# Transposing h with VectorE blocks and SBUF-to-SBUF DMAs in place of TensorE, in a fused two-layer graph kernel

## The chip, the cores and the metric

The kernel runs on one core of a Trainium2 chip. The metric is the device time of one execution in microseconds (us), as the median of several executions. A profiled execution supplies the trace; its span runs from the first to the last instruction of the core. PE is TensorE's matmul side, PEld its weight loads, DVE is VectorE, ACT is ScalarE, POOL is GpSimd, and SP is SyncE, which here only issues DMAs.

## What is computed

The input x holds 128 graphs of 128 nodes with 512 features, float32. Every graph has the same 128x128 adjacency `adj`.

```python
h = max(layernorm(x), 0)
z_l, z_g, v = h @ W_lang.T, h @ W_grav.T, h @ W_V.T
A_l = max(cosine(z_l, z_l), 0) * not_eye            # z_l normalized by its row norms
A_g = exp(-squared_distance(z_g, z_g) / (2 sigma^2)) * not_eye
K   = w_l * rownorm(A_l * adj) + (1 - w_l) * rownorm(A_g * adj)
x   = x + (K @ v) @ W_O.T
h   = max(layernorm(x), 0)
out = x + (adj * adj).T @ h + bias
```

Both similarity matrices are of the form h M h^T, with M a product of a weight and its transpose. The kernel therefore never forms z. It needs h transposed (features on the partitions) for every product of this first layer.

## The kernel before

Graphs go in groups of four (GB = 4), so there are NG = 32 groups. Every float32 operand of a matmul is split into two fp32r parts, `hi` (a copy by ScalarE) and `lo` (operand minus hi, by VectorE or GpSimd), and a product takes three passes: hi hi, hi lo, lo hi (`passes`, L185; the helper `product`, L822). So each result in PSUM is drained by a pair: ScalarE writes the hi part, VectorE subtracts it and writes the lo part.

PSUM has a ring of four banks for most results. Each result is one use of the ring. The semaphore `drained` counts uses that VectorE has emptied, in order, and `free(use)` (L811) makes TensorE wait until the use four before this one is drained.

An iteration i of the main loop does, on TensorE (L858):

- the y stage: eight blocks `y_block(a, l)` of group i, of 3, 3, 6, 6, 9, 9, 12 and 12 matmuls. They read the hi and lo parts of hT, the transposed h. Before the eighth block stand the four transposes of K of group i-1 (L834).
- the K v stage: four products `k_v` of group i-1, three matmuls each. They need the split of K transposed (`kt_lo`, L584).
- the p stage: four products of 12 matmuls with 256 columns into `p_ps`. It waits for all eight y uses to be drained (L882).
- the v stage: four products v(b) of 12 matmuls (hT times MT). Behind each v(b) the four transposes of h of graph b of group i+1 (`transposes_h`, L815) go into a ring bank. Behind v(2) come eight transposes of P (L896), which wait for `p_shifted`.
- the layer-1 stage: four products `layer1` of group i-1, three matmuls each.

So one iteration has 24 uses of the ring (PER): 8 y, 4 K v, 4 v, 4 transposed h, 4 layer 1.

VectorE's order in iteration i (L644): the eight y_lo drains, between them the row factors and `combine` of K of group i-1, four `x_stats(i+1)` (batch norm statistics of the next group's x) and `kt_lo`; then `residual(i-1)` (L588: four additions and four statistics); then for each b `v_lo(b)` and `t_lo(b)`, with the reduction to `sq` behind b = 0 and `sum_s` (L706) behind b = 2; then `output` of graphs 0, 1, 2, `similarities` (L545), `output` of graph 3 and `mask_l`.

ScalarE's order (L381): the eight y_hi copies, with `w_g_K_g` and `kt_copy` between them; `apply_norm1(i+1)` (L367: four activations that make h of the next group); two copies of p; `h2_full(i-1)` for graphs 0 and 1 (L437), which wait for GpSimd's `norm2`; then for each b the copies `v_hi(b)` and `t_hi(b)`, behind b = 0 `h2_full` of graphs 2 and 3 and `shift` (which waits for `sq`), behind b = 1 and 2 two `h2_copy` each; then the exponentials.

GpSimd's order (L312): `norm1(i+1)` (ten small steps that turn the statistics of x into scale and shift), two `add_bias(i-1)`, `norm2(i-1)` (the same ten steps for the second layer norm), `diagonal(i)`, two `add_bias`, `row_norms(i)`, and four `h2_lo(i-1)` which the layer-1 stage needs.

SP's order (L216): `load_x(i+2)`, a load of 1 MB for three slots of `x_ring`; the two small DMAs of `spread_norms(i)`; four stores of 256 KB each of group i-1.

Of the kernel before, what the change touches and what calls it, by code (L numbers as in the profile page):

```python
# [5 lines left out]
ALU = mybir.AluOpType  # L25
# [4 lines left out]

P = 128
GB = 4
SLOTS = 3
# [5 lines left out]
def gnn_pair(nc, x, adj, w_lang, w_grav, w_v, w_o, gate_logit, log_sigma, bias, out):  # L39
    B, N, D = x.shape  # L40
    assert N == P and B % GB == 0 and D % P == 0 and D <= 512 and D // P == GB
    C = D // P
# [5 lines left out]
    RN_STEPS = 2  # L48
    blk = {ac: n for n, ac in enumerate(TRI)}

    G_USES = 2 * C
    SETUP = C
    PER = G_USES + GB + 2 * GB + GB

# [3 lines left out]

    HI_PER = G_USES + 2 * GB

# [6 lines left out]
    with ExitStack() as ctx:  # L69
# [46 lines left out]
        deg = sb("deg", [P, 4, GB, 2])  # L116


        raw_l = x2[:, :, :]
# [56 lines left out]
        ln1_step, ln2_step = sem("ln1_step"), sem("ln2_step")  # L176
        h2_split_dve = sem("h2_split_dve")
        ln2_last = sem("ln2_last")
        ln2_rstd = sem("ln2_rstd")
# [9 lines left out]
        def wait_for(eng, sem, count):  # L189

            if not isinstance(count, int) or count > 0:
                eng.wait_ge(sem, count)

        block = ctx.enter_context(nc.Block())
# [3 lines left out]
        def _(sp):  # L198
# [10 lines left out]
            def spread_norms(g):  # L209
# [4 lines left out]
                sp.dma_start(rn_cols[:, :, :], rn_dram.unsqueeze(0).to_broadcast([P, P, GB])).then_inc(rn_spread, 16)  # L214

            def iteration(i, load=True, store=True, after=True):  # L216
                if load:
                    sp.wait_ge(x_loaded, 16 * i + 32)
                    if store:
                        sp.wait_ge(drained, first_use(i) + G_USES + GB)  # L220
                    else:
                        sp.wait_ge(w_split, 3 * C)
                    load_x(i + 2)
                if after:
                    spread_norms(i)
                if store:
                    store_out(i - 1, first_use(i) + PER - GB * (1 if after else 2))

# [14 lines left out]
            iteration(NG - 1, load=False, after=False)  # L243
            store_out(NG - 1, first_use(NG))
            sp.wait_ge(out_stored, 16 * GB * NG)
# [115 lines left out]
        def _(act):  # L361
# [4 lines left out]

            def apply_norm1(g, wait_free=True):  # L367
                act.wait_ge(ln1_step, LN_STEPS * (g + 1))
                if wait_free:
                    act.wait_ge(t_done, GB * g)  # L370
                for b in range(GB):
# [4 lines left out]
            def t_hi(g, b, n):  # L376
                act.wait_ge(t_done, GB * g + b + 1)
                act.activation(hT[0][:, :, b], bank(n).rearrange("p (c m) -> p c m", c=C), ACT.Copy)\
                   .then_inc(hi_ready, 1)

            def iteration(i, before=True, after=True):  # L381
# [3 lines left out]
                for a in range(C):  # L385
                    for l in range(2):
# [31 lines left out]
                for b in range(GB):  # L418
# [18 lines left out]
            def h2_full(g, b, last=False):  # L437
# [64 lines left out]
            act.activation(sig, lsig, ACT.Exp).then_inc(exp_gate, 1)  # L502
            apply_norm1(0, wait_free=False)
            lw_hi(1, side, side_hi)
            for b in range(GB):
                t_hi(0, b, SETUP + b)
            act.wait_ge(a2_step, 1)
# [14 lines left out]
        def _(dve):  # L522
# [11 lines left out]
            def x_stats(g, b0, b1):  # L534
# [108 lines left out]

            def iteration(i, before=True, after=True):  # L644
                n = 0
                hi = first_hi(i)
                for a in range(C):
                    for l in range(2):
# [32 lines left out]
                for b in range(GB):  # L681
                    hi = hi + 1
                    lo(v[1][:, b], bank(n), v[0][:, b], hi).then_inc(drained, 1)
                    n += 1
                    hi = hi + 1
# [115 lines left out]
            residual(g, 0, first_use(g) + PER - GB, last=True)  # L801
            h2_lo(g, 0)
# [7 lines left out]
        def _(pe):  # L810
# [3 lines left out]

            def transposes_h(g, b, n, use):  # L815
                pe.wait_ge(h_ready, GB * g + b + 1)
                free(use)
# [40 lines left out]
            def iteration(i, before=True, after=True):  # L858
                n, use = 0, first_use(i)

                for a in range(C):
# [27 lines left out]
                for b in range(GB):  # L889
# [4 lines left out]
                    if b == (2 if after else 0):  # L894
# [27 lines left out]
            for b in range(GB):  # L922
                transposes_h(0, b, SETUP + b, SETUP + b)
            pe.wait_ge(w_loaded["o"], 16)
# [13 lines left out]
            g = NG - 1  # L938
            use = first_use(g) + PER - GB
            pe.wait_ge(kt_split, NG)  # L940
# [28 lines left out]
```

## Time and profile before

| | |
|---|---|
| three executions | 1307.92, 1308.20, 1308.43 us; median 1308.2 |
| span of the profiled execution | 1305.4 us |
| PE busy | 1281.8 us, 98% |
| DVE, ACT, POOL busy | 71%, 54%, 47% |
| share of PE on the chain that ended last | 95% |
| DMA traffic | 80 MB, mean 61 GB/s |

The span is 2.8 us less than the median; that much lies around the profiled span. A matmul row's duration includes its latency in the array. Matmuls overlap, so their cost in a stream is the distance between two starts, or the length of a piece of the chain divided by its matmuls. The chain of work that ended last is followed backwards from the last instruction, at each step to what released it. The timeline gives starts, and the idle time and releaser in brackets.

### The profile page before, as it was taken

The numbers are of one execution on the slowest core, as the hardware profiler recorded it, in microseconds if no ns is written. First come the engines' busy times: TensorE is split into PE (matmuls) and PEld (weight loads), VectorE is DVE, ScalarE is ACT, GpSimd is POOL, SyncE is SP. The second block draws the span as 40 slices with busy tenths as digits, with TensorE's granted clock in tenths as the row PEclk, the third lists the DMA queues.
The fourth block names the chain that finished last, engine by engine and source line by source line (L and its number), as shares of the span: only waits on it lengthen the run. The fifth ranks groups of instructions, "written<-read, shape, count | busy, mean of one in ns | idle before, by whom it ended". The sixth has DMA issues, their size and how long they took to land.

```text
span 1305.4 us, 22778 instructions
## 1 busy us (share of the span) xinstructions
PE 1281.8 (98%) x6820; PEld 1094.9 (84%) x6820; DVE 924.4 (71%) x1609; ACT 708.3 (54%) x1324; POOL 610.3 (47%) x995
## 2 busy tenths in 40 slices
PE   7999999999999999999999999999999999999995
PEld 6888888888888888888888888888888888888884
DVE  5477666777666777666778666778666778666678
ACT  5445655545655545655545655545555555555534
POOL 1124555444555444455444455444455444455534
PEclk9999999999999999999999999999999999999998
DMA  5011221111221121221121221121221121221011
GB/s 204 33 31 51 73 70 43 64 68 45 72 72 40 64 72 40 72 72 40 64 72 40 72 72 40 64 72 40 72 72 41 64 71 40 72 72 51 22 41 65
DMA packets 47006, 80.02 MB, mean 61 GB/s; under 512 B 7952, under 2 KB 8080, under 8 KB 46992
## 3 DMA queue, kind: packets, MB, share of 16 engines
q1 hardware_dynamic: 46416, 79.51, 18.3%
q10 hardware_dynamic: 576, 0.33, 0.1%
q8 instruction: 8, 0.13, 0.0%
q14 instruction: 6, 0.05, 0.0%
HBM read 46.20 MB, written 33.62 MB: 61 GB/s over the span
## 4 chain that ended last, share of the span: by engine, by line
PE 95%; DVE 3%; ACT 1%; DMA 1%; issue 0%; POOL 0%; SPq 0%; DVEq 0%
PE ring L824 74%; PE p_ps L824 14%; PE ring L819 4%; PE p_ps L897 2%; PE kt_ps L837 1%; DMA h2f<-in_L_gnn_W_grav 1%; DVE x_out L642 0%; DVE hT_lo L529 0%; ACT h L373 0%; DVE bn L600 0%; DVE y_lo L746 0%; DVE x L596 0%; DVE bn L541 0%; DVE K L580 0%; DVE Lw_lo L761 0%
## 5 line engine op out<-in xcount | busy, mean ns | idle before, releaser
L529 DVE TENSOR_TENSOR v_lo<-ring,v_hi 128x512 fp32r<-128x512 f32 x128 | 88.5, 692 | 290.2 <-ACT v_hi L422 290.2
L388 ACT ACTIVATE y_hi<-ring 128x512 fp32r<-128x512 f32 x256 | 149.0, 594 | 253.1 <-PE ring L824 250.6
L264 POOL TENSOR_TENSOR ln<-bn 128x4 f32<-128x4 f32 x63 | 13.1, 208 | 546.2 <-DVE bn L541 533.1
L824 PE MATMUL ring<-hT_hi,Lw_hi 128*128 128x512 f32 x640 | 252.5, 395 | 3.1 <-DVE hT_lo L529 3.1
L824 PE MATMUL ring<-hT_hi,Lw_lo 128*128 128x512 f32 x640 | 249.7, 390 | 0.0
L824 PE MATMUL ring<-hT_lo,Lw_hi 128*128 128x512 f32 x640 | 249.1, 389 | 0.0
L824 PE MATMUL ring<-MT_hi,hT_hi 128*128 128x512 f32 x512 | 208.7, 408 | 0.0
L824 PE MATMUL ring<-MT_hi,hT_lo 128*128 128x512 f32 x512 | 201.0, 393 | 0.0
L824 PE MATMUL ring<-MT_lo,hT_hi 128*128 128x512 f32 x512 | 200.3, 391 | 0.0
L295 POOL TENSOR_TENSOR h_lo<-h2f,h_hi 128x512 fp32r<-128x512 f32 x124 | 157.9, 1295 | 57.8 <-ACT h_hi L451 57.8
L529 DVE TENSOR_TENSOR y_lo<-ring,y_hi 128x512 fp32r<-128x512 f32 x256 | 170.1, 685 | 13.2 <-ACT y_hi L388 12.8
L288 POOL TENSOR_TENSOR x_out<-x,bias_sb 128x512 f32<-128x512 f32 x128 | 163.4, 1299 | 21.4 <-DVE bn L600 19.6
L824 PE MATMUL p_ps<-y_hi,hT_lo 128*128 128x256 f32 x512 | 144.9, 283 | 0.0
L824 PE MATMUL p_ps<-y_lo,hT_hi 128*128 128x256 f32 x512 | 144.9, 283 | 0.0
L824 PE MATMUL p_ps<-y_hi,hT_hi 128*128 128x256 f32 x512 | 144.7, 283 | 0.0
L824 PEld LDWEIGHTS ring<-hT_hi,Lw_hi 128*128 128x128 f32 x640 | 120.2, 188 | 27.6 <-issue 1.9
L373 ACT ACTIVATE h<-x_ring,ln 128x512 f32 (+1 forms) x128 | 94.0, 807 | 87.9 <-POOL ln L278 87.9
L824 PEld LDWEIGHTS ring<-hT_hi,Lw_lo 128*128 128x128 f32 x640 | 120.1, 188 | 25.7
L824 PEld LDWEIGHTS ring<-hT_lo,Lw_hi 128*128 128x128 f32 x640 | 120.3, 188 | 24.2
L824 PEld LDWEIGHTS ring<-MT_hi,hT_lo 128*128 128x128 f32 x512 | 96.1, 188 | 21.5
L824 PEld LDWEIGHTS ring<-MT_lo,hT_hi 128*128 128x128 f32 x512 | 96.7, 189 | 16.5
L824 PEld LDWEIGHTS ring<-MT_hi,hT_hi 128*128 128x128 f32 x512 | 96.5, 188 | 16.3
(160 smaller groups left out, 2586.0 us busy)
## 6 DMA issues: line engine op xcount, KB each, us to landing
x_ring<-in_x SPq DMA_DIRECT2D x32, 1024.0 KB, 5.3
out<-x_out SPq DMA_DIRECT2D x128, 256.0 KB, 2.1
rn_cols<-rn_dram SPq DMA_DIRECT2D x31, 256.0 KB, 3.6
x<-in_L_gnn_W_lang SPq DMA_DIRECT2D x4, 256.0 KB, 5.5
h2f<-in_L_gnn_W_grav SPq DMA_DIRECT2D x1, 1024.0 KB, 8.9
chain<-in_L_gnn_W_O SPq DMA_DIRECT2D x1, 1024.0 KB, 12.8
x_ring<-in_L_gnn_W_V SPq DMA_DIRECT2D x1, 1024.0 KB, 14.6
rn_dram<-rn SPq DMA_DIRECT2D x31, 2.0 KB, 1.4
```

The lines of the kernel that those rows point to most:

```text
L264: pool.tensor_tensor(t[:, SUM], bn[:, :, 1], bn[:, :, 4], ALU.add).then_inc(step, 1)
L288: pool.tensor_tensor(x_out[:, b], x2[:, b], bias_sb[:, :], ALU.add).then_inc(x2b_ready, 1)
L295: pool.tensor_tensor(h2[1][:, b], h2f[:, b], h2[0][:, b].bitcast(F32), ALU.subtract)\
L373: act.activation(h[:, b], xb, ACT.Relu, bias=ln1[:, SHIFT, b:b + 1], scale=ln1[:, RSTD, b:b + 1]).then_inc(h_ready, 1)
L388: act.activation(y[0][:, a, :, l], bank(n).rearrange("p (b m) -> p b m", b=GB), ACT.Copy)\
L529: return dve.tensor_tensor(out, ps, part(hi), ALU.subtract)
L819: mm = pe.transpose(bank(n)[:, c * P:(c + 1) * P], h[:, b, c * P:(c + 1) * P], ident[:, :])
L824: mm = pe.matmul(out, lhsT, rhs, start=(k == 0), stop=(k == len(terms) - 1))
L837: mm = pe.transpose(kt_ps[:, b], K[:, b], ident[:, :])
L897: mm = pe.transpose(p_ps[:, k // 2, k % 2], P_sb[:, k // 2, k % 2], ident[:, :])
```

## The change

h of the next group is no longer transposed by TensorE inside the main loop. (Group 0 still is.)

- `normalize` replaces `apply_norm1` on ScalarE: the four activations of group i+1 stand in the y stage, two behind y_hi(5), two behind y_hi(6) and `kt_copy`.
- `turn_blocks` on VectorE: four instructions per group, each transposing one graph's 128x512 in 32x32 blocks. Two stand around `kt_lo` between y_lo(6) and y_lo(7), two behind y_lo(7). They write into the buffer of h2f, which `h2_full` uses later in the same iteration.
- `turn_h` on SP, first in the iteration: when all four blocks are ready, sixteen DMAs, each of 32 partitions by 512 elements (64 KB), which carry block row i to block column j, into the new buffer `h_turned`.
- `turned_hi` and `turned_lo` take the places of `t_hi` and `t_lo` and read `h_turned` in SBUF, not PSUM. `turned_hi(b)` waits for the DMAs and for v(b), whose operand it overwrites.
- `h2_full(i-1, 0)` waits for the sixteen DMAs of group i+1.
- `x_stats` of group i+2 moves from the y stage to the v stage: two behind `sum_s` (b = 2), two behind `turned_lo(3)`, both ahead of `output`.
- The ring has 20 uses per iteration; TensorE waits for `ht_lo` at the start of each iteration.

```diff
-    PER = G_USES + GB + 2 * GB + GB
+    PER = G_USES + GB + GB + GB
...
+        h_turned = sb("h_turned", [P, NQ, C * GB * Q])
+        h_blocks = h2f[:, :, :].rearrange("p b d -> p (b d)").rearrange("p (j e) -> p j e", j=NQ)
...
+            def turn_h(g):
+                sp.wait_ge(blocks_ready, GB * g)
+                for i in range(NQ):
+                    for j in range(NQ):
+                        sp.dma_start(h_turned[j * Q:(j + 1) * Q, i], h_blocks[i * Q:(i + 1) * Q, j])\
+                          .then_inc(turned, 16)
+
             def iteration(i, load=True, store=True, after=True):
+                if after:
+                    turn_h(i + 1)
...
+            def turned_hi(g, b):
+                if b == 0:
+                    act.wait_ge(turned, TURN * g)
+                act.wait_ge(v_done, GB * (g - 1) + b + 1)
+                act.activation(hT_columns(0, b), h_columns(b), ACT.Copy).then_inc(ht_hi, 1)
...
+                        if after and G_USES - 2 <= n < G_USES:
+                            normalize(i + 1, (n - G_USES + 2) * GB // 2)
...
-                if after:
-                    apply_norm1(i + 1)
...
                     if after:
-                        t_hi(i + 1, b, n)
-                        n += 1
+                        turned_hi(i + 1, b)
...
                 if b == 0:
                     wait_for(act, h2_split, GB * g)
+                    act.wait_ge(turned, TURN * (min(g + 2, NG - 1) if isinstance(g, int) else g + 2))
...
+            def turn_blocks(g, b):
+                if b == 0 and not (isinstance(g, int) and g < 3):
+                    dve.wait_ge(h2_split, GB * (g - 2))
+                dve.wait_ge(h_ready, GB * g + b + 1)
+                out = h_blocks.rearrange("p j (c b q) -> p c b j q", c=C, b=GB)[:, :, b]
+                dve.transpose(out, h[:, b].rearrange("p (c j q) -> p c j q", c=C, j=NQ)).then_inc(blocks_ready, 1)
+
+            def turned_lo(g, b):
+                dve.wait_ge(ht_hi, GB * (g - 1) + b + 1)
+                dve.tensor_tensor(hT_columns(1, b), h_columns(b), part(hT_columns(0, b)), ALU.subtract)\
+                   .then_inc(ht_lo, 1)
...
-                        if n == G_USES - 2:
-                            if before and after:
-                                x_stats(i + 1, 0, GB // 2)
-                            if before:
-                                kt_lo(i - 1)
-                            if before and after:
-                                x_stats(i + 1, GB // 2, GB)
-                        if not before and n == G_USES:
-                            x_stats(i + 1, 0, GB)
+                        if after and n >= G_USES - 1:
+                            turn_blocks(i + 1, 2 * (n - G_USES + 1))
+                        if before and n == G_USES - 1:
+                            kt_lo(i - 1)
+                        if after and n >= G_USES - 1:
+                            turn_blocks(i + 1, 2 * (n - G_USES + 1) + 1)
...
-                    t_lo(b, n, hi).then_inc(drained, 1 if before or b < GB - 1 else 1 + GB)
-                    n += 1
+                    turned_lo(i + 1, b)
...
                     if b == 2:
                         sum_s(i)
+                    if stats and b >= 2:
+                        x_stats(i + 2, (b - 2) * GB // 2, (b - 1) * GB // 2)
...
+            x_stats(1, 0, GB)
             iteration(0, before=False)
             iteration(1)
-            with dve.Fori(2, NG - 1) as i:
+            with dve.Fori(2, NG - 2) as i:
                 iteration(i)
+            iteration(NG - 2, stats=False)
...
                 n, use = 0, first_use(i)
-
+                wait_for(pe, ht_lo, GB * i)
...
-                    if after:
-                        transposes_h(i + 1, b, n, use + n)
-                        n += 1
```

## Rows read from the trace of the kernel before

**Rows 1.** The page: busy time of TensorE; the chain that ended last, by engine.
```profile
PE 1281.8 (98%) x6820; PEld 1094.9 (84%) x6820; DVE 924.4 (71%) x1609; ACT 708.3 (54%) x1324; POOL 610.3 (47%) x995
...
PE 95%; DVE 3%; ACT 1%; DMA 1%; issue 0%; POOL 0%; SPq 0%; DVEq 0%
```
**Rows 2.** The chain in order of time, 638 to 680 us: start us, us, what.
```profile
646.53 0.44 PE ring L819 x4
...
652.94 0.87 PE p_ps L897 x8
...
657.45 13.65 PE ring L824 x60
...
671.54 5.49 PE ring L824 x24
```
**Rows 3.** The transposes of h by their line: duration ns min/median/max.
```profile
L819 PE MATMUL ring<-ident,h x512: 270/272/299, 23.1 to 1242.2; 128*128 128x128 f32 x171
```
**Rows 4.** The timeline of PE: start us, us; the first matmul of K v.
```profile
635.15 0.39 PE L824 MATMUL ring<-v_hi,KT_hi 128*128 128x512 f32 x1
```
**Rows 5.** The timeline of DVE, 630 to 662 us: start us, us, idle before.
```profile
631.43 1.28 DVE L541 BATCH_NORM_STATS2 bn<-x_ring 128x6 f32 x2
633.29 0.69 DVE L586 TENSOR_TENSOR KT_lo<-kt_ps,KT_hi 128x512 fp32r<-128x512 f32 x1 [0.58 <-ACT KT_hi L473]
...
635.98 0.69 DVE L529 TENSOR_TENSOR y_lo<-ring,y_hi 128x512 fp32r<-128x512 f32 x1 [0.21 <-ACT y_hi L388]
...
640.16 1.28 DVE L600 BATCH_NORM_STATS2 bn<-x 128x6 f32<-128x512 f32 x2
...
648.40 1.21 DVE L693 TENSOR_REDUCE sq<-chain 128x8 f32<-128x1024 f32 x1
...
655.52 1.22 DVE L708 TENSOR_TENSOR chain<-p_ps,chain 128x1024 f32<-128x1024 f32 x1
...
658.88 1.88 DVE L642 TENSOR_TENSOR x_out<-ring,x_out 128x512 f32<-128x512 f32 x3
```
**Rows 6.** The timeline of ACT, 635 to 656 us.
```profile
638.74 2.94 ACT L373 ACTIVATE h<-x_ring,ln 128x512 f32 x4 [2.79 <-POOL ln L278]
...
644.78 1.52 ACT L444 ACTIVATE h2f<-x,ln 128x512 f32<-128x512 f32 x2 [0.37 <-POOL ln L278]
646.57 0.60 ACT L422 ACTIVATE v_hi<-ring 128x512 fp32r<-128x512 f32 x1 [0.26 <-PE ring L824]
...
649.65 1.28 ACT L456 ACTIVATE chain<-chain,sq 128x128 f32<-128x128 f32 x4 [0.59 <-DVE sq L693]
650.84 0.58 ACT L422 ACTIVATE v_hi<-ring 128x512 fp32r<-128x512 f32 x1
...
651.79 1.14 ACT L451 ACTIVATE h_hi<-h2f 128x512 fp32r<-128x512 f32 x2
```
**Rows 7.** The timeline of POOL, 641 to 648 us.
```profile
641.52 0.21 POOL L264 TENSOR_TENSOR ln<-bn 128x4 f32<-128x4 f32 x1 [0.42 <-DVE bn L600]
...
644.70 2.40 POOL L302 TENSOR_TENSOR chain<-chain,diag_of 128x1024 f32<-128x1024 f32 x1
```
**Rows 8.** The timeline of SP at the start of the span.
```profile
0.81 1.81 SPq L231 DMA_DIRECT2D x<-in_L_gnn_W_lang  x4
```
**Rows 9.** SP's stores by their line: duration of an issue, ns min/median/max.
```profile
L206 SPq DMA_DIRECT2D out<-x_out x128: 332/333/349, 113.6 to 1303.0; - x128
```
**Rows 10.** The page, DMA issues: KB each, median us from issue to landing.
```profile
x_ring<-in_x SPq DMA_DIRECT2D x32, 1024.0 KB, 5.3
out<-x_out SPq DMA_DIRECT2D x128, 256.0 KB, 2.1
...
rn_dram<-rn SPq DMA_DIRECT2D x31, 2.0 KB, 1.4
```
**Rows 11.** The chain in order of time, near both ends of the span.
```profile
74.95 11.15 PE ring L824 x48
...
1242.45 13.65 PE ring L824 x60
```

More of the change, by code:

```diff
@@ L31 @@
 P = 128
+Q = 32
 GB = 4
@@ L49, in gnn_pair @@
     blk = {ac: n for n, ac in enumerate(TRI)}
+    NQ = P // Q
+    TURN = 16 * NQ * NQ
+    assert C == NQ
     G_USES = 2 * C
     SETUP = C
-    PER = G_USES + GB + 2 * GB + GB
+    PER = G_USES + GB + GB + GB
     def first_use(i):
         return SETUP + GB + PER * i
-    HI_PER = G_USES + 2 * GB
+    HI_PER = G_USES + GB
     def first_hi(i):
@@ L177, in gnn_pair @@
         h2_split_dve = sem("h2_split_dve")
+        blocks_ready, turned = sem("blocks_ready"), sem("turned")
+        ht_hi, ht_lo = sem("ht_hi"), sem("ht_lo")
         ln2_last = sem("ln2_last")
@@ L192, in wait_for, with h_columns, hT_columns @@
                 eng.wait_ge(sem, count)
+        def h_columns(b):
+            return h_turned[:, :, :].rearrange("p i (c b q) -> p c b i q", c=C, b=GB)[:, :, b]
+        def hT_columns(part, b):
+            return hT[part][:, :, b].rearrange("p c (i q) -> p c i q", q=Q)
         block = ctx.enter_context(nc.Block())
@@ L226, in iteration @@
                 if store:
-                    store_out(i - 1, first_use(i) + PER - GB * (1 if after else 2))
+                    store_out(i - 1, first_use(i) + PER - GB)
             w_rows = w_lang.rearrange("(c p) n -> p c n", p=P)
@@ L243, in _ @@
             iteration(NG - 1, load=False, after=False)
-            store_out(NG - 1, first_use(NG))
+            store_out(NG - 1, first_use(NG) + GB)
             sp.wait_ge(out_stored, 16 * GB * NG)
@@ L365, in _, with normalize @@
             act.dma_start(bias_sb[:, :], bias.unsqueeze(0).to_broadcast([P, D])).then_inc(consts_loaded, 16)
[L367 to L371, printed above, removed]
+            def normalize(g, b0):
+                if b0 == 0:
+                    act.wait_ge(ln1_step, LN_STEPS * (g + 1))
+                    if isinstance(g, int) and g == 1:
+                        act.wait_ge(t_done, GB)
+                    elif not isinstance(g, int) or g > 1:
+                        act.wait_ge(blocks_ready, GB * (g - 1))
+                for b in range(b0, b0 + GB // 2):
                     xb = x_ring[:, bass.ds(g % SLOTS, 1), b].rearrange("p s d -> p (s d)")
@@ L374, in apply_norm1, with t_hi @@
                                    scale=ln1[:, RSTD, b:b + 1]).then_inc(h_ready, 1)
-            def t_hi(g, b, n):
-                act.wait_ge(t_done, GB * g + b + 1)
+            def t_hi(b, n):
+                act.wait_ge(t_done, b + 1)
                 act.activation(hT[0][:, :, b], bank(n).rearrange("p (c m) -> p c m", c=C), ACT.Copy)\
                    .then_inc(hi_ready, 1)
+            def turned_hi(g, b):
[3 more added lines that the diff above has]
+                act.activation(hT_columns(0, b), h_columns(b), ACT.Copy).then_inc(ht_hi, 1)
             def iteration(i, before=True, after=True):
@@ L502, in _ @@
             act.activation(sig, lsig, ACT.Exp).then_inc(exp_gate, 1)
-            apply_norm1(0, wait_free=False)
+            normalize(0, 0)
+            normalize(0, GB // 2)
             lw_hi(1, side, side_hi)
             for b in range(GB):
-                t_hi(0, b, SETUP + b)
+                t_hi(b, SETUP + b)
             act.wait_ge(a2_step, 1)
@@ L642, in output, with iteration @@
                 dve.tensor_tensor(x_out[:, b], bank(n), x_out[:, b], ALU.add).then_inc(drained, 1)
-            def iteration(i, before=True, after=True):
+            def iteration(i, before=True, after=True, stats=True):
                 n = 0
@@ L682, in iteration @@
                     hi = hi + 1
-                    lo(v[1][:, b], bank(n), v[0][:, b], hi).then_inc(drained, 1)
+                    lo(v[1][:, b], bank(n), v[0][:, b], hi)\
+                        .then_inc(drained, 1 if before or b < GB - 1 else 1 + GB)
                     n += 1
-                    hi = hi + 1
-                    t_lo(b, n, hi).then_inc(drained, 1 if before or b < GB - 1 else 1 + GB)
-                    n += 1
+                    turned_lo(i + 1, b)
                     if b == 0:
@@ L793, in _ @@
             dve.tensor_tensor(A2[1][:, :], adj2[:, :], part(A2[0][:, :]), ALU.subtract).then_inc(a2_step, 1)
+            x_stats(1, 0, GB)
             iteration(0, before=False)
             iteration(1)
-            with dve.Fori(2, NG - 1) as i:
+            with dve.Fori(2, NG - 2) as i:
                 iteration(i)
+            iteration(NG - 2, stats=False)
             iteration(NG - 1, after=False)
             g = NG - 1
-            residual(g, 0, first_use(g) + PER - GB, last=True)
+            residual(g, 0, first_use(NG), last=True)
             h2_lo(g, 0)
@@ L813, in free, with transposes_h @@
                 wait_for(pe, drained, use - BANKS + 1)
-            def transposes_h(g, b, n, use):
-                pe.wait_ge(h_ready, GB * g + b + 1)
+            def transposes_h(b, n, use):
+                pe.wait_ge(h_ready, b + 1)
                 free(use)
@@ L922, in _ @@
             for b in range(GB):
-                transposes_h(0, b, SETUP + b, SETUP + b)
+                transposes_h(b, SETUP + b, SETUP + b)
             pe.wait_ge(w_loaded["o"], 16)
@@ L938, in _ @@
             g = NG - 1
-            use = first_use(g) + PER - GB
+            use = first_use(NG)
             pe.wait_ge(kt_split, NG)
```

## The prediction

> **What bounds the kernel now.** I read the busy times first, then the chain that ended last, then one iteration in the timelines. TensorE is busy for 98% of the span and holds 95% of the chain [rows 1]. In the steady part its stream has no gap: the chain in order of time is PE alone [rows 2]. So work taken from TensorE is worth its full length, until something else is late. Group 1's y stage begins at 74.95, group 31's at 1242.45 + 2.75 (three matmuls of each of four layer-1 products come first) [rows 11]. That is 1170.2 us for 30 iterations, 39.0 us each. The span is 1305.4 us against a median of 1308.2; I work on the span and add 2.8 us at the end.
>
> I count time in an iteration from the first K v matmul (t = 0, at 635.15) [rows 4]. The y stage takes 48 matmuls at 13.65 / 60 = 0.2275 us, 10.9, plus 0.44 for the transposes of K (the hole between the two last pieces) plus half of 5.49 [rows 2]: 14.1 us. So the next y stage begins at t = 24.9 before the change.
>
> **What is removed.** The transposes of h are 16 matmuls for each of 31 groups in the loop (512 in all with group 0's) [rows 3]. Their duration is 272 ns each, but they overlap: on the chain four take 0.44 us [rows 2]. Four such fours are 1.76 us an iteration. With no new wait the period is 37.24 us, the y stage begins at t = 23.1, and the kernel takes 1308.2 - 31 x 1.76 = about 1254 us. That is the most the change can give.
>
> **The DVE transposes.** No row shows one. An ordinary DVE pass over 512 elements is issued every 0.60 us (two in 1.28, three in 1.88) [rows 5]; a pass over 1024 elements takes 1.21. The transpose reads and writes 512 elements per partition, so it is nearest to the first; I take 0.60, and 1.20 as the upper end. Nothing makes it cheaper than a plain pass, so 0.60 is also the lower end. The Trainium skill (VectorE: DVE Perf Modes, The three transpose paths) gives 311 ns for a VectorE transpose of 128x128 bf16, not of float32. Four of those would be 1.24 us, the upper end, if its fixed part came each time. No run here shows it yet.
>
> The two that stand before y_lo(7) replace statistics of the same length, and are hidden: `kt_lo` ended at 633.98, and moved behind y_lo(6) and one transpose it ends at 634.65, still 0.5 us before K v. y_lo(7) starts at t = 0.83 as before [rows 5]. The two behind it stand ahead of `residual` and move it by 1.2 us. Its last statistics ended at 641.44, t = 6.3 [rows 5]; now 7.5. GpSimd's ten steps of norm2 began then, at 641.52, and released `h2_full` at 644.78, 3.26 later [rows 6, 7]. So `h2_full` of graphs 0 and 1 can begin at t = 10.8, no longer at 9.6.
>
> **The sixteen DMAs.** They start when the last block is ready, t = 2.7. Each costs SP an issue: 0.333 us [rows 9], and four in a row took 1.81, 0.45 each [rows 8]. I take 0.38 (the issue plus a gap of 0.05), because 128 stores spread over the whole span stand against four loads at its start, and the longest of the stores is 0.349. The last is issued at 2.8 + 15 x 0.38 = 8.5. From issue to landing 2 KB took 1.4 us and 256 KB took 2.1 [rows 10]; a 64 KB one lies between, so they have landed at t = 9.9 to 10.6. A load of the same 1 MB in one DMA took 5.3 us [rows 10], so the engines aren't the limit. That is just before 10.8: the DMAs are hidden behind norm2, with 0.2 to 0.9 us to spare. At 0.45 an issue and 2.1 to land it is t = 11.7, and 0.9 us shows. The Trainium skill (DMA: Bandwidth & Descriptors, Anatomy of one DMA) puts a DMA at about 2.0 us plus bytes / 436 GB/s for the GpSimd path: by it 64 KB take 2.15 us, t = 10.65, hidden by 0.15. Its section Bandwidth warns of transfers under 64 KB as descriptor-dominated and would have one of 1 MB; sixteen small ones are the opposite.
>
> Behind the sixteen on SP stands `load_x(i+2)`, then issued at t = 8.9, landing at 14.2. VectorE's statistics of that group come at 21.8, so this is free. The spread of the norms waits for GpSimd's step behind sq, at about 17, after both. The four activations of h move to idle ScalarE time, between y_hi(5) and y_hi(7); 2.94 us [rows 6]. Two take 1.5 us beside a y block of 9 or 12 matmuls (2.0 or 2.7 us), of which the copy takes 0.6: free. ScalarE's wait of 2.79 us for norm1 goes, and norm1 has the whole y stage: free.
>
> **The path through ScalarE and VectorE.** This is where I expect the loss. A copy on ScalarE is issued every 0.49 us from PSUM, 0.57 from SBUF, an h2_full every 0.74 [rows 6].
> - ScalarE: two `h2_full` at 10.8, v_hi(0) at 12.3, turned_hi(0) at 12.8, two `h2_full` at 13.35 to 14.8.
> - VectorE: v_lo(0) at 12.9, turned_lo(0) at 13.5, the reduction to sq at 14.1; `shift` follows it by 1.25 [rows 5, 6], at 15.4. The diagonal, 2.40 us behind norm2 [rows 7], is ready at 13.2 and isn't waited for. P's transposes need `shift` by 16.7; it ends at 16.6.
> - ScalarE, back to back: v_hi(1) 16.6, turned_hi(1) 17.1, two `h2_copy` 17.65, v_hi(2) 18.8, turned_hi(2) 19.3.
> - VectorE: v_lo(2) 19.4, turned_lo(2) 20.0, sum_s 20.6 to 21.8 (1.22) [rows 5], **two statistics** to 23.0, v_lo(3) 23.0, turned_lo(3) 23.6, **two statistics** 24.2 to 25.4, output of graph 0 until 26.05.
>
> The first y block reuses the bank of layer 1 of graph 0 (four uses back), so it waits for that output, although hT's lo part is ready at 24.3. Before, the outputs stood directly behind t_lo(3): the first ended at 659.56, t = 24.4 [rows 5], 0.5 us before the y stage. That slack is gone, the y stage would be ready 1.76 us sooner, and 2.4 us of statistics are put ahead of the output. It begins at t = 26.1 rather than 23.1: a stall of 3.0 us. Part of it shows already at layer 1, whose fourth product waits for v_lo(3) until 23.7. What is queued behind these instructions on VectorE (outputs 1 and 2, similarities, output 3, mask_l) costs the fourth y block 0.1 us more. The y stage is then 14.2 and the period 40.3 us, against 39.0.
>
> **The sum.** Iteration 0 has no outputs: it loses its transposes and keeps the wait for ht_lo(3), so group 1 begins at 73.5 instead of 74.95. Twenty-nine periods of 40.3 are 1168.7. Iteration 30 has no statistics: its outputs begin at 23.0, and layer 1, waiting for h2's lo parts, ends at about 24.1; with the y stage 38.3. From there to the end nothing is changed: 1305.4 - 1245.2 = 60.2. Together 1340.7, plus 2.8: **1343.5 us**, 2.7% slower.
>
> **Rivals.**
> - **The drains aren't late** (faster). If ScalarE keeps pace with TensorE, v(3) is ready at 20.5, v_lo(3) starts at 21.2, turned_lo(3) at 21.8, the statistics at 22.4, output 0 ends at 24.2. The stall is 1.2 us, the period 38.5, the sum 1290 us. It needs ScalarE 1.8 us ahead of my schedule; its chain starts from norm2, which the moved residual makes later, so the profile speaks against it. A chance of 0.17, with 0.03 of it for no stall at all (1254).
> - **The break-even point** is a stall of 1.75 us, output 0 done at 24.85. Chance of landing there 0.04.
> - **The DMAs land late** (slower still). From t = 10.8 on, each us of lateness delays `h2_full`, v_hi(0) and everything after them by one us. At t = 11.7 to 11.9, 1 us: period 41.3, 1372 us. For it: the spacing at the start of the trace, and that no SBUF-to-SBUF transfer is in it. Chance 0.18.
> - **A DVE transpose takes two passes.** 0.6 more each: `kt_lo` ends 0.1 late for K v, y_lo(7) starts 0.4 later, residual 1.2 more. Norm2, and the DMAs too, come 1.6 us later: 29 x 1.6 = 47, 1390 us. Chance 0.13.
>
> **Range and chances.** My forecast's own case has 0.48 and reaches from 1325 to 1360 (0.5 us an iteration either way). The break-even chance is split over the three. Faster 0.18, within 0.2% 0.02, slower 0.80; 0.2% is about what a measurement of this kernel can tell from no change. For 8 in 10 the range takes in 1290 below and 1390 above and leaves the gain without a stall out.
>
> **What would show it.** In the changed profile TensorE should wait about 3 us in each of 29 iterations, mostly at the first y block, released by VectorE's output (x_out), with smaller waits at layer 1 for v_lo and h_lo. ScalarE's `h2_full` should be released by GpSimd's norm2; if it is a DMA, the DMA rival holds, and its excess is the lateness. A VectorE transpose should last about 0.68 us, issued every 0.60. SP should issue the sixteen in about 6 us. I am wrong if output 0 comes less than 1.7 us behind the last layer-1 product, if TensorE's waits sum to under 50 us, or if the DMAs' landing, not norm2, sets the start of `h2_full` by more than a us.

## The result, and the profile after

The changed kernel takes 1469.8 us (median of four, 1468.9 to 1472.0), against 1308.1 us for the kernel before: a ratio of 1.124, 95% interval 1.1225 to 1.1257. Slower was forecast, but 1343.5 us with a range from 1290 to 1390; the loss is 162 us and not 35.

The page of the changed kernel: busy times, the chain that ended last by engine, and the new DMAs (KB each, median us from issue to landing). The chain was 95% PE before [rows 1].

```profile
PE 1292.6 (88%) x6324; PEld 1065.8 (73%) x6324; DVE 1020.4 (70%) x1733; ACT 702.0 (48%) x1324; POOL 652.7 (44%) x995
...
PE 34%; SPq 18%; DVE 16%; issue 13%; ACT 12%; DMA 5%; DVEq 2%; ACTq 0%; POOL 0%
...
h_turned<-h2f SPq DMA_DIRECT2D x496, 64.0 KB, 2.0
```

SP's queue holds 18% of the chain. A queue that only issues DMAs has become a link of it. The waits of the engines (us in total, times, longest) name who waits for what:

```profile
ACT h2f L458 <- DMA h_turned<-h2f: 150.1, 30, 5.8
...
PE p_ps L923 <- ACT chain L470: 98.9, 31, 4.0
...
PE ring L850 <- DVE x_out L669: 40.8, 30, 1.4
...
PE ring L850 <- DVE v_lo L544: 7.8, 26, 0.7
```

ScalarE's `h2_full` waits for the sixteen DMAs in 30 iterations, and TensorE waits in front of the transposes of P and at the first y block. One iteration follows in the timelines of PE, SP and ACT. The first K v matmul starts at 621.50; that is t = 0.

```profile
621.50 0.39 PE L850 MATMUL ring<-v_hi,KT_hi 128*128 128x512 f32 x1
...
641.57 1.11 PE L923 MATMUL p_ps<-ident,chain 128*128 128x128 f32 x8 [3.25 <-ACT chain L470]
...
642.91 0.63 PE L850 MATMUL ring<-MT_lo,hT_hi 128*128 128x512 f32 x1
...
651.62 0.50 PE L850 MATMUL ring<-hT_hi,Lw_hi 128*128 128x512 f32 x1 [1.42 <-DVE x_out L669]
```
```profile
624.26 10.04 SPq L216 DMA_DIRECT2D h_turned<-h2f  x16
634.90 0.40 SPq L196 DMA_DIRECT2D x_ring<-in_x  x1
```
```profile
635.75 1.52 ACT L458 ACTIVATE h2f<-x,ln 128x512 f32<-128x512 f32 x2 [4.98 <-DMA h_turned<-h2f]
```

The sixteen issues start at t = 2.76, as worked out, but take 10.04 us, 0.63 each. `h2_full` starts at t = 14.25, where norm2 alone would have let it start at 10.8. The next y stage begins at t = 30.1; before the change it began at 24.9 [rows 2, 4]. The period is 44.4 us.

VectorE in the same iteration:

```profile
622.94 1.29 DVE L563 STREAM_TRANSPOSE h2f<-h 128x512 f32<-128x512 f32 x2
...
638.40 0.68 DVE L567 TENSOR_TENSOR hT_lo<-h_turned,hT_hi 128x512 fp32r<-128x512 f32 x1
...
644.68 1.57 DVE L567 TENSOR_TENSOR hT_lo<-h_turned,hT_hi 128x512 fp32r<-128x512 f32 x1
```

The block transposes cost what a plain pass costs (1.29 us for two, [rows 5] 1.28). The same `turned_lo` (hT_lo) takes 0.68 us once and, for b = 2, 1.57. The matmul at 642.91 lasts 0.63 us where others last 0.39. The row of that stretch (us busy of PE, PEld, DVE, ACT and POOL, then the granted clock as a share of full speed, the DMA share and GB/s) says why:

```profile
641.60:646.10 4.50, 4.50 (x17) 3.72 (x18) 3.31 (x4) 4.01 (x8) 3.17 (x4) 0.62 0.30 48
```

The granted clock is at its lower level (1.2 in place of 2.4 GHz) for 3.4 us in most iterations, behind TensorE's wait of 3.25 us; over these 4.5 us that makes a mean of 0.62.

### The profile page after: what moved, and what is told of

It reads as the page before. It is cut to its first block, busy times and chain, and to the rows that moved or that the text cites. A ratio compares the mean times of both kernels' runs of the same rounds, so it can differ in the third digit from the quotient of the medians.

```text
span 1468.0 us, 22296 instructions
## 1 busy us (share of the span) xinstructions
PE 1292.6 (88%) x6324; PEld 1065.8 (73%) x6324; DVE 1020.4 (70%) x1733; ACT 702.0 (48%) x1324; POOL 652.7 (44%) x995
## 4 chain that ended last, share of the span: by engine, by line
PE 34%; SPq 18%; DVE 16%; issue 13%; ACT 12%; DMA 5%; DVEq 2%; ACTq 0%; POOL 0%
PE ring L850 33%; SPq L216 18%; DVE bn L556 4%; DMA h_turned<-h2f 4%; ACT v_hi L436 3%; DVE sq L715 3%; DVE chain L732 2%; ACT h_hi L465 2%; ACT chain L470 2%; ACT h2f L458 2%; DVE h2f L563 2%; DVE x_out L669 1%; DVE hT_lo L567 1%; ACT y_hi L402 1%; ACT hT_hi L393 1%
## 5 line engine op out<-in xcount | busy, mean ns | idle before, releaser
L850 PE MATMUL ring<-hT_hi,Lw_hi 128*128 128x512 f32 x640 | 257.7, 403 | 44.3 <-DVE x_out L669 40.8
L850 PE MATMUL ring<-MT_hi,hT_hi 128*128 128x512 f32 x512 | 217.9, 426 | 0.0
L850 PE MATMUL ring<-MT_lo,hT_hi 128*128 128x512 f32 x512 | 214.1, 418 | 0.0
L850 PE MATMUL ring<-MT_hi,hT_lo 128*128 128x512 f32 x512 | 212.8, 416 | 0.0
L300 POOL TENSOR_TENSOR h_lo<-h2f,h_hi 128x512 fp32r<-128x512 f32 x124 | 172.0, 1418 | 45.2 <-ACT h_hi L465 45.2
L458 ACT ACTIVATE h2f<-x,ln 128x512 f32<-128x512 f32 x128 | 97.1, 805 | 159.1 <-DMA h_turned<-h2f 150.1
L424 ACT ACTIVATE chain<-p_ps 128x512 f32<-128x512 f32 x64 | 38.3, 598 | 230.2 <-PE p_ps L850 230.2
L923 PE MATMUL p_ps<-ident,chain 128*128 128x128 f32 x256 | 38.2, 296 | 98.9 <-ACT chain L470 98.9
L850 PEld LDWEIGHTS ring<-MT_hi,hT_lo 128*128 128x128 f32 x512 | 104.7, 205 | 23.9
L850 PEld LDWEIGHTS ring<-MT_hi,hT_hi 128*128 128x128 f32 x512 | 105.9, 207 | 21.5
```

Of the source, the lines that this page charges most:

```text
L300: pool.tensor_tensor(h2[1][:, b], h2f[:, b], h2[0][:, b].bitcast(F32), ALU.subtract)\
L424: act.activation(P_sb[:, 2 * half:2 * half + 2], p_ps[:, 2 * half:2 * half + 2], ACT.Copy)\
L850: mm = pe.matmul(out, lhsT, rhs, start=(k == 0), stop=(k == len(terms) - 1))
L923: mm = pe.transpose(p_ps[:, k // 2, k % 2], P_sb[:, k // 2, k % 2], ident[:, :])
```

## The experiments

Three theories stood against each other: the sixteen issues on one queue; the order of the work on VectorE (statistics ahead of the outputs); and VectorE and GpSimd hindering each other, or TensorE's clock.

**What an issue costs.** `e_issue` is the kernel before with small DMAs behind its end. Two of its nine groups:

```diff
+            for k in range(4):
+                sp.dma_start(dst[32:64, k], src[0:32, k]).then_inc(trial, 16)
+            landed(4)
...
+            for k in range(4):
+                sp.dma_start(trial_dram[32 * k:32 * k + 32], src[0:32, k]).then_inc(trial, 16)
+            landed(4)
```

> The kernel before with a row of small DMAs behind the last store, four of each form and then a wait until they have landed: 32 partitions by 2 KB within SBUF to another quarter of the partitions, to the same quarter, in the last quarter; 128 partitions by 512 bytes, by 2 KB and by 1 KB within SBUF; 32 partitions by 2 KB from SBUF to DRAM and back; and sixteen in the pattern of the change. The question is why an issue takes 0.59 us (0.63 apart) where a store of 128 rows takes 0.333. If the form with 32 partitions costs it, the 32-partition forms show 0.59 and those of 128 partitions 0.33. If SBUF on both sides costs it, all forms within SBUF show 0.59 and the stores to DRAM 0.33. If it is only the queue filling up, the first DMA of each four is at 0.33 and the later ones at 0.59.

SP's timeline. L257 to L269 are the first five forms, L272 goes to DRAM, L275 comes from it, L278 is the one by 1 KB, L282 the sixteen:

```profile
1305.82 2.56 SPq L257 DMA_DIRECT2D h<-x_ring  x4
1309.82 2.43 SPq L260 DMA_DIRECT2D h<-x_ring  x4
1313.71 2.90 SPq L263 DMA_DIRECT2D h<-x_ring  x4
1318.07 2.47 SPq L266 DMA_DIRECT2D h<-x_ring  x4
1321.91 2.44 SPq L269 DMA_DIRECT2D h<-x_ring  x4
1326.29 1.77 SPq L272 DMA_DIRECT2D trial_dram<-x_ring  x4
1329.38 1.70 SPq L275 DMA_DIRECT2D h<-trial_dram  x4
1332.59 2.43 SPq L278 DMA_DIRECT2D h<-x_ring  x4
1336.54 10.09 SPq L282 DMA_DIRECT2D h<-x_ring  x16
```

Every form within SBUF takes about 0.61 us an issue (one group of four 0.73), whether 32 or 128 partitions, 64 or 256 KB, and sixteen in a row take 0.63 each. With DRAM on one side it is 0.43 to 0.44, for the same 32 partitions by 2 KB. So SBUF on both sides costs it, not the shape. The rows of single issues show a second, smaller effect: the first of a burst is cheap (0.312 and 0.366 us with DRAM, 0.49 to 0.54 within SBUF), the later ones are not (0.42 and 0.59 to 0.60). The 0.333 us of the stores [rows 9] were issues that each stood alone.

**Eight issues on each of two queues.**

```diff
-                for i in range(NQ):
+                for i in range(NQ // 2):
...
+            def turn_half(g):
+                act.wait_ge(blocks_ready, GB * g)
+                for i in range(NQ // 2, NQ):
+                    for j in range(NQ):
+                        act.dma_start(h_turned[j * Q:(j + 1) * Q, i], h_blocks[i * Q:(i + 1) * Q, j])\
+                           .then_inc(turned, 16)
...
+                if after:
+                    turn_half(i + 1)
```

> The changed kernel with eight of the sixteen DMAs issued by ScalarE's queue (between its last y copy and its first copy of p) and eight by SP. Theory 1, the issue on one queue: sixteen issues 0.63 us apart land the blocks at t = 14.2 (t counted from the first K v matmul), 3.4 us after norm2 releases h2_full at 10.8; with eight they land at about 2.8 + 7 x 0.63 + 2.0 = 9.2, the wait of h2_full on the DMAs (150 us in total) goes, each of 29 periods falls from 44.4 by about 3.4 to 4.1 us, and so do TensorE's waits in front of the transposes of P; 1470 - 29 x 3.8 = about 1360 us, and the low clock in each iteration disappears too. Rival A, the DMA engines themselves are slow with 32-partition transfers: the landing comes no earlier than before, and the time stays near 1470. Rival B, the lateness is set elsewhere (the statistics in front of the outputs): under 1.5 us an iteration are won, 1425 or more.

1409.9 us, ratio 1.078 (1.0758 to 1.0794): 2.0 us an iteration won, not 3.8. The cause held (`h2_full` is now released by GpSimd), the size didn't. The timelines of ACT and DVE and two pieces of the chain of this kernel (its t = 0 is at 641.76):

```profile
652.66 1.52 ACT L467 ACTIVATE h2f<-x,ln 128x512 f32<-128x512 f32 x2 [1.64 <-POOL ln L283]
```
```profile
655.31 1.40 DVE L576 TENSOR_TENSOR hT_lo<-h_turned,hT_hi 128x512 fp32r<-128x512 f32 x1
...
662.32 1.61 DVE L576 TENSOR_TENSOR hT_lo<-h_turned,hT_hi 128x512 fp32r<-128x512 f32 x1
```
```profile
625.91 12.80 PE ring L859 x48
...
669.28 11.29 PE ring L859 x48
```

`h2_full` starts at t = 10.9, as the prediction had it, 3.35 us sooner than in the changed kernel. Of that, 0.7 us goes to turned_lo(0), which now takes 1.40 us. And in 13 of 30 iterations a low stretch of the clock falls into the y stage, where nothing covers it: 48 matmuls take 12.80 us instead of 11.29. That is 1.5 us each time (2.4 in one), 0.7 on average: the periods are 41.8 us without such a stretch and 43.4 with it. 3.35 - 0.7 - 0.7 is 1.95, against 2.0 measured.

**The same megabyte in four DMAs.** `q_four` leaves out the move of the blocks to other partitions, so it doesn't compute the kernel's result; the bytes moved and the work of the compute engines are the same.

```diff
-    TURN = 16 * NQ * NQ
+    TURN = 16 * NQ
...
-                for i in range(NQ):
-                    for j in range(NQ):
-                        sp.dma_start(h_turned[j * Q:(j + 1) * Q, i], h_blocks[i * Q:(i + 1) * Q, j])\
-                          .then_inc(turned, 16)
+                for j in range(NQ):
+                    sp.dma_start(h_turned[:, j], h_blocks[:, j]).then_inc(turned, 16)
```

> The changed kernel with the sixteen DMAs of 64 KB replaced by four of 256 KB on SP, 128 partitions each: the same megabyte within SBUF with four issues. The blocks are not moved to other partitions, so the transposed h is wrong and the output isn't the reference's; the work of every engine is as before. If the number of issues (0.63 us each within SBUF) made the landing late, the blocks land at 2.8 + 3 x 0.63 + 2.5 = 7.2, h2_full is released by norm2 at t = 10.8, and the first y block starts at t = 26.1 of the prediction plus 1.4 for two turned_lo that run beside GpSimd: about 27.5, period 41.7, 1385 us, and up to 1410 with the lower clock that the run with two queues still had. If the megabyte itself is slow within SBUF, h2_full still waits for the DMAs and the time stays near 1470.

1408.2 us, ratio 1.077 (1.0755 to 1.0791), the same as with two queues, and within what was expected. The bytes are equal, the issues take 2.42 us instead of 10.04, and the wait for the DMAs is gone. With `e_issue`, where 32 and 128 partitions cost the same, this settles it: the number of issues on one queue made the landing late, not the megabyte, and ScalarE's part in `a_split` costs nothing.

```profile
641.69 2.42 SPq L215 DMA_DIRECT2D h_turned<-h2f  x4
```
```profile
649.83 1.52 ACT L456 ACTIVATE h2f<-x,ln 128x512 f32<-128x512 f32 x2 [1.62 <-POOL ln L281]
```

**The statistics ahead of the outputs**, first with the moves alone. In `d_moves` TensorE keeps its transposes.

```diff
+                        if after and G_USES - 2 <= n < G_USES:
+                            normalize(i + 1, (n - G_USES + 2) * GB // 2)
...
-                if after:
-                    apply_norm1(i + 1)
...
-                            if before and after:
-                                x_stats(i + 1, 0, GB // 2)
...
+                    if stats and b >= 2:
+                        x_stats(i + 2, (b - 2) * GB // 2, (b - 1) * GB // 2)
```

> The kernel before with TensorE's transposes kept, and only the two moves of the change: h's activations in the y stage, and the next statistics in the v stage in front of the outputs. If the statistics in front of the outputs hold up the first y block as the prediction had it, output 0 ends at t = 26.8 instead of 24.4, the y stage begins 1.9 us late in 29 iterations: 1308 + 55 = 1363 us. If the whole loss is the DMAs', the moves cost nothing: 1308 us, and the wait of TensorE on x_out stays under 5 us in total.

1340.2 us, ratio 1.0245 (1.0228 to 1.0262): the moves alone cost 32 us, 1.1 us in each of 29 iterations. The first y block waits for output 0. DVE's v_lo(3) in the kernel before, DVE here, and a wait of PE here:

```profile
657.68 0.69 DVE L529 TENSOR_TENSOR v_lo<-ring,v_hi 128x512 fp32r<-128x512 f32 x1 [0.94 <-ACT v_hi L422]
```
```profile
673.64 0.67 DVE L530 TENSOR_TENSOR v_lo<-ring,v_hi 128x512 fp32r<-128x512 f32 x1
...
674.83 1.27 DVE L542 BATCH_NORM_STATS2 bn<-x_ring 128x6 f32 x2
676.02 1.87 DVE L643 TENSOR_TENSOR x_out<-ring,x_out 128x512 f32<-128x512 f32 x3
```
```profile
PE ring L822 <- DVE x_out L643: 21.0, 29, 0.7
```

v_lo(3) has no idle time in front of it here. In the kernel before, VectorE waited 0.94 us there for ScalarE; the first two statistics fill that hole. 1.9 expected less 0.9 is 1.0: the y stage begins 0.9 us later than before, and it takes 0.2 us more itself.

`b_split_stats` moves the statistics of the two-queue kernel out of that place. The edit against `a_split`:

```diff
-                    if stats and b >= 2:
-                        x_stats(i + 2, (b - 2) * GB // 2, (b - 1) * GB // 2)
+                    if stats and b < 2:
+                        x_stats(i + 2, b * GB // 2, (b + 1) * GB // 2)
```

> As the one before (eight DMAs on each of two queues), and the four statistics of the group after next stand on VectorE behind sq (b = 0) and behind turned_lo(1), where VectorE waits anyway, not in front of the outputs. Theory 1 with the prediction's second term, that 2.4 us of statistics ahead of output 0 hold up the first y block: the period falls by another 2.4 us, to about 38.5, and the kernel takes about 1290 us, below the kernel before. Rival, that the first y block waits for something else (hT's lo part, the lo parts of h2): under 1 us an iteration is won, 1330 us or more.

1340.4 us, ratio 1.025 (1.0232 to 1.0266): 69 us less than `a_split`, 2.3 us an iteration. That this is nearly the 2.4 us of the four statistics is luck; two things make it up. The y stage begins 1.8 us sooner (t = 25.7 against 27.5): 2.4 less 0.6, since turned_lo(3) now runs beside GpSimd. In `a_split` and here:

```profile
666.76 0.68 DVE L576 TENSOR_TENSOR hT_lo<-h_turned,hT_hi 128x512 fp32r<-128x512 f32 x1
```
```profile
673.73 1.28 DVE L576 TENSOR_TENSOR hT_lo<-h_turned,hT_hi 128x512 fp32r<-128x512 f32 x1
```

And the low stretches of the clock in the y stage are gone, 0.7 us on average. The time expected was 50 us lower because it started from 1360 for the kernel with two queues.

**VectorE beside GpSimd.** `f_pool_cut` is `b_split_stats` with GpSimd's two large operations cut to 8 columns; it leaves out the rest of the bias and of the lo part of h2. The first of the two:

```diff
-                pool.tensor_tensor(x_out[:, b], x2[:, b], bias_sb[:, :], ALU.add).then_inc(x2b_ready, 1)
+                w = D if isinstance(g, int) else 8
+                pool.tensor_tensor(x_out[:, b, 0:w], x2[:, b, 0:w], bias_sb[:, 0:w], ALU.add).then_inc(x2b_ready, 1)
```

> b_split_stats with GpSimd's two large operations in the loop (x_out <- x + bias, and the lo part of h2) cut from 512 to 8 columns; the rest of those tiles is left as it was, so part of the output isn't computed. Theory: VectorE's turned_lo, which since the change has both inputs in SBUF, is slowed where GpSimd works in SBUF beside it (rows of 1.26 to 1.40 us against 0.68). Then all turned_lo are at 0.68 here, and about 1.9 us an iteration on VectorE's path go, part of it hidden: the time falls from 1340 to 1290 to 1310 us. Rival: the long rows come from a wait within the instruction for something else (ScalarE's write, the DMAs): they stay at 1.3 us with GpSimd idle.

1281.2 us in a single execution, 59 us under `b_split_stats` and below the range expected. The 124 `turned_lo` by their line (ns min/median/max), in `b_split_stats` and in `f_pool_cut`, then GpSimd's `h2_lo` in `b_split_stats`:

```profile
L576 DVE TENSOR_TENSOR hT_lo<-h_turned,hT_hi x124: 681/1268/1606, 63.7 to 1274.3; 128x512 fp32r<-128x512 f32 x124
```
```profile
L578 DVE TENSOR_TENSOR hT_lo<-h_turned,hT_hi x124: 679/682/1340, 63.8 to 1217.7; 128x512 fp32r<-128x512 f32 x124
```
```profile
L300 POOL TENSOR_TENSOR h_lo<-h2f,h_hi x124: 1279/1338/1747, 108.5 to 1314.9; 128x512 fp32r<-128x512 f32 x124
```

The median falls from 1268 to 682 ns. `t_lo` read PSUM and SBUF; `turned_lo` reads two operands in SBUF, and waits for GpSimd's instruction there. In `a_split`, turned_lo(2) starts at 662.32 within an `h2_lo` that ends at 663.38, and ends 0.55 us behind it; the next `h2_lo` then takes 1.74 us in place of 1.3. The Trainium skill (SBUF — State Buffer, SBUF: two separate sides) has this rule: a VectorE operation with two SBUF inputs and a GpSimd operation that reads SBUF exclude each other for a whole instruction. The trace agrees. Three of four `turned_lo` were long in `b_split_stats`; they are 1.8 us an iteration shorter in all, and the period falls by 1.9, from 40.0 to 38.1. But the run also takes GpSimd's h_lo off TensorE's path, so not all of the 59 us need be the contention.

**Order along the path.** `g_spread` is `b_split_stats` with three block transposes, not two, ahead of y_lo(7), where VectorE was idle.

```diff
-                        if after and n >= G_USES - 1:
-                            turn_blocks(i + 1, 2 * (n - G_USES + 1))
+                        if after and n == G_USES - 2:
+                            turn_blocks(i + 1, 0)
+                        if after and n == G_USES - 1:
+                            turn_blocks(i + 1, 1)
...
-                            turn_blocks(i + 1, 2 * (n - G_USES + 1) + 1)
+                            turn_blocks(i + 1, n - G_USES + 3)
```

> b_split_stats with the first three block transposes ahead of y_lo(7) (behind y_lo(5), behind y_lo(6), behind kt_lo) and only the fourth behind it. The prediction's step that each transpose ahead of residual moves norm2, h2_full and everything behind it by 0.6 us, one for one, to the first y block: 0.6 us an iteration less, 1340 - 18 = 1322 us. Rival: the chain behind norm2 isn't what ends last, the time stays at 1340.

1321.2 us, ratio 1.010 (1.0084 to 1.0117): 19 us, 0.64 an iteration for one transpose of 0.6. The chain behind norm2 is passed on one for one.

`n_best` adds two changes of order: turned_lo(0) stands behind the reduction to sq, and GpSimd's first three `add_bias` stand ahead of norm2, so that only one of them is left to run beside VectorE's work on b = 0. The edit against `g_spread`:

```diff
-                    turned_lo(i + 1, b)
                     if b == 0:
                         dve.wait_ge(diag_ready, i + 1)
...
                         dve.tensor_scalar(sqc[:, :], sq[:, :, 0], EPS * EPS, None, ALU.max).then_inc(sq_ready, 1)
+                    turned_lo(i + 1, b)
...
-                    for b in range(GB // 2):
-                        add_bias(i - 1, b)
+                    for b in range(GB - 1):
+                        add_bias(i - 1, b, first_use(i) + G_USES)
```

> g_spread with two more changes of order: on VectorE the reduction to sq stands in front of turned_lo(0), not behind it, and GpSimd adds the bias to graphs 0, 1 and 2 ahead of norm2 as soon as x2 is drained, so that one and not two of these run beside turned_lo(0). If the chain norm2, h2_full, v_hi(0), sq, shift, ScalarE's copies is what makes the first y block late, shift comes 1.3 us sooner, and the time falls by 0.8 to 1.4 us an iteration against g_spread, to 1280 to 1300 us, under the kernel before. If VectorE's mere amount of work between sq and output 0 is the limit, under 0.4 us an iteration are won, 1310 us or more.

1284.5 us, ratio 0.982 (0.9802 to 0.9835): 1.8% faster than the kernel before, with the change's own means, and 37 us less than `g_spread`. The two changes were not tried apart. TensorE's waits that come back in every iteration are down to this:

```profile
PE ring L863 <- POOL h_lo L303: 8.9, 30, 0.3
```

The first matmul of layer 1, in the kernel before and in `n_best` (whose t = 0 is at 625.26):

```profile
657.21 0.47 PE L824 MATMUL ring<-h_hi,A_hi 128*128 128x512 f32 x1
```
```profile
645.58 0.39 PE L863 MATMUL ring<-h_hi,A_hi 128*128 128x512 f32 x1
```

That is t = 22.06 and t = 20.32: up to there the iteration is shorter by the transposes, and without a stall. The row of waits shows only part of what is left: layer 1 takes 3.7 us from its start to the y stage, before the change 2.85, and the y stage 0.2 us more than before. The period is 38.25 us, 1.0 more than the 37.24 that the prediction gave for no new wait.

`p_best_sp` gives all sixteen issues back to SP in that kernel (`turn_half` is no longer called, `turn_h` has its full range again).

> n_best with all sixteen DMAs issued by SP again, none by ScalarE. They start at t = 2.1 there and land at 2.2 + 15 x 0.63 + 2.0 = 13.7, where n_best's h2_full starts at t = 10.3. If the lateness of the landing is passed on one for one to the first y block, the loop loses 3.4 us less the slack that n_best has (TensorE waits there for 0.3 us an iteration at layer 1 only): 2.4 to 3.4 us in 30 iterations, 1284 + 72 to 102 = 1356 to 1386 us. If ScalarE's early copies matter less than I think, under 1.5 us an iteration: below 1330 us.

1389.6 us, ratio 1.063 (1.0614 to 1.065): 105 us for the place of eight issues, 3.5 us an iteration, just above the range expected. `h2_full` starts at t = 13.66 against 10.29 in `n_best`, 3.37 us later, and the y stage 3.46 later: the lateness is passed on whole, with no slack taken off. Thirteen low stretches of the clock came with it in the loop, in the v stage; they cost nothing (periods of 41.8 us with one and 41.7 without). ACT waits for the DMAs again:

```profile
645.19 1.52 ACT L467 ACTIVATE h2f<-x,ln 128x512 f32<-128x512 f32 x2 [4.38 <-DMA h_turned<-h2f]
```

**The clock in the changed kernel.** `l_filled` keeps TensorE busy where it waited.

```diff
+                        if after:
+                            product(r_ps[:, :, :].rearrange("p b m -> p (b m)"), [t for c in range(C) for t in passes(
+                                [w[:, c, 3] for w in hT], [w[:, c] for w in MT])])
                         pe.wait_ge(p_shifted, i + 1)
```

> The changed kernel as it is, with one product more (twelve matmuls of 512 columns, 2.75 us) into an unused bank in front of the transposes of P, where TensorE waits 3.2 us for shift. The result of it is not used. Theory: the wait of some 3 us lets the granted clock fall to its lower level for 3.4 us in each iteration (28 such stretches in the trace of the changed kernel), and the work behind it, on the path, takes 1.5 to 1.7 us longer. With TensorE kept busy the low stretches go and the kernel gets faster by 30 x 1.6 = 48 us, to about 1420. Rival: the slow stretch isn't on the path, since VectorE's outputs end last; the time stays at 1470, or rises if the added work pushes something.

1475.7 us, ratio 1.1285 (1.1266 to 1.1304), 6 us more than the changed kernel. The low stretches are all but gone (4 instead of 26, 19 us instead of 100 in all), but nothing is won: my theory fell and the rival held. The y stage begins at t = 30.1 as before and the period is 44.4 us as before; nearly all of the 6 us lie in the first iterations. The waits of PE show why:

```profile
PE ring L850 <- DVE x_out L669: 41.4, 30, 1.4
...
PE p_ps L926 <- ACT chain L470: 18.6, 31, 1.6
```

The first y block waits for output 0 as long as before, on VectorE. In the changed kernel the slow stretch lies in the v stage, ahead of that wait, which takes up what it costs. In `a_split` it lies in the y stage and costs 1.5 us each time. What it costs depends on where it lies.

## Why the prediction was wrong, point by point

- **What bounds the kernel, and what the transposes are worth.** Right. Freed of the new waits, `n_best` runs with PE at 97% and 1249.0 us busy, 33 us less than before, as it holds none of the loop's 496 transposes of h. Its layer 1 starts 1.74 us sooner; the sum has 1.76.
- **The block transposes.** Right: 0.69 us, issued every 0.60. The upper end of 1.20 was not needed, and the rival of two passes fell. The Trainium skill (VectorE: DVE Perf Modes, The three transpose paths) gives 311 ns for 128x128 bf16; four times that, 1.24 us, was an estimate for 512 columns, and the trace of float32 has 0.69.
- **norm2 and h2_full at t = 10.8.** Right: 10.9 in `a_split`, in `g_spread` 0.6 us less.
- **The sixteen DMAs: the step that failed.** The landing time was right (2.0 us; the bounds were 1.4 to 2.1), the start too. The issue was taken at 0.38 us; it is 0.63. Two mistakes lie in it, both of reading rows. The 0.333 of [rows 9] belong to issues that stand alone, and the burst in [rows 8] already said 0.45; I set it aside as an effect of the start. That is 15 x 0.07 = 1.0 us. And no row had SBUF on both sides; I extrapolated from DRAM rows and took 0.45 as the upper bound. That is 15 x 0.18 = 2.7 us. Together 3.7; the blocks landed at t = 14.2 instead of 9.9 to 10.6, so they and not norm2 set the start of `h2_full`, 3.45 us late. The prediction had named this as a sign of being wrong.
- **The rival of the late DMAs** had the mechanism and its rule, one for one from t = 10.8 on, but its price was 1 us an iteration, 1372 us, where it is 3.4. The range's upper end of 1390 came from the rival of the two-pass transpose and was too low for the same reason. `p_best_sp` measures the place of eight issues alone at 3.5.
- **turned_lo at the cost of t_lo.** Wrong in size: 1.57 us for turned_lo(2), 0.9 more, on the path. I looked at how many inputs there are and not at where they lie. Predicted 26.1, plus 3.45 for the DMAs, plus 0.9, is 30.45; measured 30.1. The 0.3 lies in ScalarE's steps, which were taken a little long: v_hi(2) came 7.7 us behind `h2_full` and not 8.0 (two `h2_copy` hold the engine for 1.04 us, not 1.15).
- **The statistics ahead of the outputs.** Right in kind: the first y block waits for x_out. By `a_split` against `b_split_stats` their place is worth 1.8 us of the start of the y stage, not the 2.4 of their length, and by `d_moves` 0.9 in the order of the kernel before.
- **P's transposes just in time.** It hung on 0.1 us, and with `h2_full` late TensorE waits there 3.25 us. TensorE's longest wait is not what sets the time, though: in `l_filled` matmuls that nobody needs fill most of it, and the y stage begins no sooner and no later.
- **The clock** wasn't in the prediction. It costs next to nothing in the changed kernel, and about 0.7 us an iteration in `a_split`.

The sum of 1343.5 with the right issue cost would have been 1343.5 + 29 x 3.45 = 1444, and with turned_lo's 0.9 us it would have been 1470. That this meets the 1469.8 to within a us is partly luck. The period is 4.1 us longer than predicted (44.4 against 40.3), which is 119 us in 29 iterations; iteration 30, left out of that sum, is 4.4 us longer; the remaining 3 us lie in single iterations and at the ends.

## What to carry to other kernels

Count the issues of a moved transfer as work of the queue, at the burst price of that kind of transfer, and place the last one's landing against the first instruction that needs it; bytes were not the matter here, sixteen issues were. When an operand moves from PSUM to SBUF, look at what GpSimd does at that time. A stall of the bounding engine points at a chain of short waits elsewhere, and reordering that chain (125 us from `a_split` to `n_best`, the lost low stretches of the clock included) was worth more than the work that the change removed (55 us). `p_best_sp` and `n_best` differ only in who issues eight DMAs, and lie on either side of the kernel before.

## What the runs showed of the hardware

- In `e_issue` an issue within SBUF takes 0.59 to 0.60 us in a burst (0.63 apart), one with DRAM on one side 0.42 (0.44 apart), and the first of a burst 0.05 to 0.12 us less; within SBUF, partitions (32 or 128) and bytes (64 to 256 KB) make no difference. ScalarE's queue has the same price (eight in 5.04 us, `a_split`).
- A `turned_lo` of 128x512, both inputs in SBUF, takes 1.26 to 1.61 us beside a GpSimd operation in SBUF (`b_split_stats`, `a_split`), 0.68 without (`f_pool_cut`).
- A VectorE transpose of 128x512 float32 in 32x32 blocks takes 0.69 us, as long as a plain pass.
- After a wait of 3.25 us TensorE's granted clock was at 1.2 GHz for 3.4 us in the changed kernel; with the wait filled (`l_filled`) it stayed at 2.4 but for two such stretches in the loop.
